# Second layer: each spread, gather, weighting and state release gets its own slot; three engines share the semaphore offsets

## The reference

```python
xa = _ln(x)                                   # then sx = shift(xa) - xa
xxx = jnp.tanh((xa + sx * maa_x) @ maa_w1)    # "hidden", then five mixes
xm = xa[:, :, None] + sx[:, :, None] * (maa_stack + xxx @ maa_w2)
w = exp(-exp(time_decay + jnp.tanh(xw @ td_w1) @ td_w2))
r, k, v, g = xr @ Wr.T, xk @ Wk.T, xv @ Wv.T, silu(xg @ Wg.T)
def step(s, rkvw):                            # over 256 positions
    a = k_t[..., :, None] * v_t[..., None, :]
    out = jnp.einsum('bhi,bhij->bhj', r_t, u * a + s)
    s = a + w_t[..., :, None] * s
    return (s, out)
og = group_norm(out) * g
x1 = x + og @ Wo.T                            # then a feed-forward block:
return x1 + sigmoid(xr2 @ Wfr.T) * (square(relu(xk2 @ Wfk.T)) @ Wfv.T)
```

## Time and profile before

| what | us |
|---|---|
| median of three runs | 4477.55 (4476.36 to 4478.06) |
| the profiled execution's own time | 4474.41 |
| its span, first to last instruction | 4472.4 |
| TensorE busy in the span | 4190.4 |
| VectorE busy | 2937.5 |
| ScalarE busy | 1965.8 |
| GpSimd busy | 1575.5 |

### The profile page before, as it was taken

One profiled execution on the slowest core, in us unless ns is written; L12 is line 12 of the kernel. 1 busy time (PEld: TensorE's weight loads), 2 busy tenths in 40 slices (PEclk: granted clock), 3 DMA queues, 4 the chain that ended last, 5 costly groups with the idle time before them and its releaser, 6 DMA issues. The chain is left out here.

```text
span 4472.4 us, 70619 instructions
## 1 busy us (share of the span) xinstructions
PE 4190.4 (94%) x22096; PEld 3152.1 (70%) x22096; DVE 2937.5 (66%) x6494; ACT 1965.8 (44%) x3814; POOL 1575.5 (35%) x1082
## 2 busy tenths in 40 slices
PE   7999999678999997699999999999999999999999
PEld 3444444356777774488887797887887977888866
DVE  5666665268888887376774775765775756757743
ACT  2555555222333331255553455552555553555522
POOL 1223233146555563133233423333333234232230
PEclk8999999889999998899999999999999999999999
DMA  1000000200000000222222312222312122222122
GB/s 40 25 20 30 20 20 15 118 5 10 15 15 15 15 10 19 74 67 67 72 62 69 102 58 76 67 67 69 98 57 81 58 69 93 63 80 73 51 81 97
DMA packets 128411, 239.77 MB, mean 54 GB/s; under 512 B 16932, under 2 KB 40100, under 8 KB 126896
## 3 DMA queue, kind: packets, MB, share of 16 engines
q1 hardware_dynamic: 126544, 232.99, 16.6%
q0 software_dynamic: 1008, 3.67, 0.2%
q10 hardware_dynamic: 624, 0.18, 0.0%
HBM read 220.79 MB, written 15.73 MB: 53 GB/s over the span
## 5 line engine op out<-in xcount | busy, mean ns | idle before, releaser
L1929 POOL TENSOR_TENSOR c_wl<-c_wr,c_wh 128x512 fp32r<-128x512 f32 (+1 forms) x576 | 819.9, 1435 | 1696.6 <-ACT c_wh L2262 1393.3
L2363 ACT ACTIVATE c_pr<-c_ps,c_nms 128x257 f32<-128x257 f32 x512 | 244.1, 477 | 484.0 <-DVE c_nms L2584 481.7
L581 ACT ACTIVATE a_ex<-a_ps 128x1024 f32<-128x1024 f32 x256 | 261.1, 1023 | 259.8 <-PE a_ps L416 259.7
L692 DVE TENSOR_REDUCE a_nm<-a_ps 128x2 f32<-128x1024 f32 x256 | 311.4, 1221 | 80.9 <-PE a_ps L393 80.8
L1521 DVE TENSOR_TENSOR_SCAN b_sb<-b_wt,b_s,b_ps 128x256 f32<-128x256 f32 x512 | 360.0, 730 | 3.5 <-issue 1.7
L1473 POOL TENSOR_TENSOR b_sb<-b_sb,b_rt 128x1024 f32<-128x1024 f32 x128 | 278.0, 2178 | 185.8 <-DVE b_sb L1521 185.8
L2262 ACT ACTIVATE c_wh<-c_wr 128x512 fp32r<-128x512 f32 (+1 forms) x464 | 315.3, 687 | 47.5 <-PE c_ps L1991 43.5
L1989 PE MATMUL c_ps<-c_hh,c_wh 128*128 128x512 f32 x768 | 310.9, 405 | 12.7 <-DVE c_hl L2468 12.4
L1989 PE MATMUL c_ps<-c_gh,c_wh 128*128 128x512 f32 x768 | 307.2, 400 | 7.1 <-DVE c_gl L2646 4.1
L1991 PE MATMUL c_ps<-c_hh,c_wl 128*128 128x512 f32 x768 | 304.9, 397 | 0.0
L1990 PE MATMUL c_ps<-c_hl,c_wh 128*128 128x512 f32 x768 | 304.3, 396 | 0.0
(11 more groups left out here) (328 smaller groups left out, 10601.8 us busy)
## 6 DMA issues: line engine op xcount, KB each, us to landing
c_wr<-in_downs SPq DMA_DIRECT2D x192, 256.0 KB, 2.7
c_wr<-in_wv SPq DMA_DIRECT2D x64, 512.0 KB, 3.9
c_wr<-in_wk SPq DMA_DIRECT2D x128, 256.0 KB, 2.9
c_wr<-in_wq SPq DMA_DIRECT2D x128, 256.0 KB, 2.6
c_wr<-in_fc SPq DMA_DIRECT2D x64, 256.0 KB, 2.8
b_w<-in_w SPq DMA_DIRECT2D x8, 1024.0 KB, 14.2
a_x<-in_x SPq DMA_DIRECT2D x8, 512.0 KB, 3.9
a_ctx<-in_ctx SPq DMA_DIRECT2D x8, 512.0 KB, 4.2
```

The costliest lines, as they stand in the source:

```text
L581: act.activation(EX[:, n % 4, :, :], ps[:, BT + 2 * (n % 2):BT + 2 * (n % 2) + 2, :], ACT.Exp).then_inc(ex_ready, 1)
L692: dve.tensor_reduce(NM[:, s, :].rearrange("p (h c) -> p h c", h=HG)[:, 2 * p:2 * p + 2, c:c + 1], ps[:, bank:bank + 2, :], AX.X, ALU.max, ...
L1929: pool.tensor_tensor(piece(WL, slot), piece(WR, slot), piece(WH, slot), ALU.subtract).then_inc(piece_cut[slot], 1)
L2363: act.activation(PR[:, i, 0:L + 1], ps[:, BS + 1 - i % 2, 0:L + 1], ACT.Exp, bias=NMS[:, i:i + 1], scale=float(K2) ** -0.5, accum_out=RS[: ...
```

## The change

Four things are changed.

1. The spreads, gathers, weighings and states of the second layer no longer have a formula: each has a slot of its own in a table of 32, 8, 16 and 16 numbers. The two sums have their own as well, and the multiply moves from 4 n - 3 to 4 n - 1.
2. All other numbers of the four tables are new too.
3. `start_ahead` is split in layers 0, 1 and 2: TensorE adds to every third semaphore, VectorE to the next, GpSimd to the rest, after its memsets.
4. In the third layer, SyncE's first context transfer and its six first weight fetches no longer wait.

```diff
@@ layers 0, 1 and 2: tensor, vector, gpsimd (after its memsets)
-            start_ahead(pe, sems)
+            start_ahead(pe, sems[0::3])
+            start_ahead(dve, sems[1::3])
+            start_ahead(pool, sems[2::3])
@@ layer1, tables
-        PE_AT = dict(spread=-29, gather=3, mean=-178, var=-142, hidden=-122, mix=(-119, -116, -114, -103, -98, -86, -80, -73, -67, -56),
...
+        PE_AT = dict(
+                     spread=(-39, -36, -35, -34, -31, -30, -16, -15, -13, -11, -8, -7, -6, 12, 13, 16, 21, 24, 34, 35, 36, 41, 43, 44, 49, 53, 57, 59, 66, 69, 81, 85),
+                     gather=(-13, -10, 18, 39, 47, 60, 91, 107), mean=-180, var=-144, hidden=-130,
...
@@ layer1, loops over the slots
-                    b = due(slot, 4 * pr + PE_AT["spread"])
+                    b = due(slot, PE_AT["spread"][pr])
...
-                    b = due(slot, 16 * o + PE_AT["gather"])
+                    b = due(slot, PE_AT["gather"][o])
...
-                    b = due(slot, 8 * q + POOL_AT["weigh"])
+                    b = due(slot, POOL_AT["weigh"][q])
@@ layer2, sync
-                sp.wait_ge(ct_ready, b + AHEAD)
-                sp.sem_inc(passed, 1)
+                if b > 0:
+                    sp.wait_ge(ct_ready, b + AHEAD)
+                    sp.sem_inc(passed, 1)
...
-                sp.wait_ge(piece_cut[slot], count + AHEAD)
-                sp.sem_inc(passed, 1)
+                if not first:
+                    sp.wait_ge(piece_cut[slot], count + AHEAD)
+                    sp.sem_inc(passed, 1)
```

More of the change, by code:

```diff
@@ L989, in layer1 @@
-        POOL_AT = dict(weigh=-20, scale=-142, shift=-135, mix=(-124, -116, -86, -69, -64), rk=(-82, -71), gate=-44, gated=133, scale2=178,
-                       shift2=189)
-        DVE_AT = dict(multiply=-3, sums=80, mean=-127, inverse=-115, blend=-108, mix=(-98, -96, -91, -81, -66, -61, -54, -47, -41, -30),
-                      v=(-32, -26), gm=(144, 146), ginverse=154, bb=(159, 162), wo=(180, 188), mean2=192, inverse2=200, fkin=221, frin=225,
-                      fv=(262, 270), out=276)
@@ L1640, in _ @@
                 for i in range(2):
-                    b = due(slot, 64 * i + DVE_AT["sums"])
+                    b = due(slot, DVE_AT["sums"][i])
                     if b is not None:
```

34 lines of the change are left out of this document (22 added, 12 removed).

## The result

| kernel | median us | runs | lowest to highest |
|---|---|---|---|
| before | 4476.36 | 5 | 4473.71 to 4478.06 |
| changed | 4454.17 | 5 | 4447.10 to 4454.75 |

The changed kernel is 22.2 us faster: ratio 0.9946, 95% interval 0.9933 to 0.9960. Its profiled execution is the fastest of its five, 4447.10 (span 4445.4), so against the 4474.41 of the profile before 27.3 us are to be placed. The medians differ by 22.2, so 5 of the 27.3 belong to that one execution.

The account below looks back on a forecast made before the run. TensorE was taken to bound the middle batches, VectorE the last, serial chains around them. Terms -4.0 - 0.5 - 3.0 - 11.5 - 5.4 + 5.5 - 2.5 = -21.4 gave 4453.0, as a median 4456; range 4441 to 4472.

Parts of the forecast that it names:

- batches 1 and 2: Second layer: eight more scans done early bring VectorE earlier to v, mean and var; -3.0 us, bounds 0 and -10.
- five middle batches: Second layer: period from hidden to hidden falls to 106.2 us, 2.3 less; -11.5 in all, bounds -20 and -1.
- last batch: Second layer, bound by VectorE: fewer scans and multiplies remain when g ends; -5.4 us, bounds -2 and -8.
- tail, scans' end to gm: Last batch: fkin stands behind seven more scans and two multiplies, so its chain ends later; +5.5 us, bounds +3 and +9.
- start of the third layer: Without SyncE's waits the first transfer and x come earlier, and the mean decides; -2.5 us, bounds -1.0 and -3.4.
- Part 1: Offsets shared by three engines: second layer's first mean 7.0 us earlier, constants hold part back, -4.0; third layer -2.5.
- Part 3: Middle batches: g to hidden becomes 22.7 to 24.9 us, hidden to g 81.6 plus new waits of 0 to 1.8; -11.5.
- Rival A: TensorE never waits in the middle: five periods of 104.3 us, 4447 in all; chance 0.17.
- rival B: The middle keeps its pace, chain and new waits replacing the old: period 108.3 us, 4467 in all; chance 0.22.
- Rival C: Slower: TensorE waits 3.5 us each middle batch at the second gather, then runs at lower clock; 4494; chance 0.04.
- Rival D: The offsets don't help: GpSimd's additions or queues shared with x hold both layer starts; 4463; chance 0.10.
- Rival E: Blend on VectorE meets GpSimd's weighings in the second layer: +4.5 us, 4461; chance 0.07.

Follow-up runs that it names:

- offsets_only: The kernel before with its own slots, plus only the shared offsets and the third layer's removed waits: 4467.67 us, ratio 0.9979 to the kernel before.
- constants_later: The changed kernel with VectorE's work on the constants behind the first batch's reciprocal instead of ahead: 4450.19 us, ratio 0.9936 to the kernel before.
- mean_later: The changed kernel with VectorE's mean of the next batch behind three more scans and a multiply: 4472.20 us, ratio 0.9995 to the kernel before.
- tables_only: The changed kernel's new slots, but TensorE adds all offsets and the third layer's waits stay: 4460.39 us, ratio 0.9961 to the kernel before.
- spreads_again: The changed kernel with four spreads issued twice in each of batches 1 to 6: 4453.84 us, ratio 0.9951 to the kernel before.
- vector_7_gathers_late: The changed kernel with four extra VectorE reciprocals and the last two gathers later on TensorE, all in the last batch: 4452.68 us, ratio 0.9951.

## Why the prediction was right, point by point

The forecast was 4456, the median is 4454.2. The terms, in the profiled execution:

| term | predicted | measured | where |
|---|---|---|---|
| start of the second layer | -4.0 | -3.7 | first transfer to hidden, 30.9 to 27.2 |
| first batch's chain | -0.5 | -0.2 | first to second hidden |
| batches 1 and 2 | -3.0 | -2.5 | second to third hidden; about 0 in six other profiles |
| five middle batches | -11.5 | -13.7 | third to eighth hidden |
| last batch | -5.4 | -7.1 | +3.1 to g, -10.2 for the scans |
| tail, scans' end to gm | +5.5 | +6.1 | |
| behind gm | 0 | +2.5 | lower clock in var2 and fk; -0.4 to -0.1 in three other profiles |
| start of the third layer | -2.5 | -1.7 | last `out` to mean |
| behind that mean | 0 | -3.4 | -4.7 in offsets_only; other meetings of VectorE with GpSimd |
| first layer | 0 | -3.3 | mostly the clock of this execution |

**In part luck: the sum.** The measured terms make -27.0 and the forecast ones -21.4. The median is within 2 us of the forecast although the profile's terms are 6 us beyond it, since the profiled execution was 7 us faster than the median. By the runs of the two halves, the slots gave 17.1 us (14.9 forecast) and the offsets 9.8 (6.5 forecast). A term that was not there (batches 1 and 2) stands against one that was not foreseen (behind the third layer's mean), while the start of the second layer and the middle came out in size (-3.7 for -4.0, -13.7 for -11.5).

**Right, and shown.** Part 1: the mean came as soon as x had landed, and the constants stopped half of that gain; constants_later gives it back. Part 3: of the two pieces of a period the first went from 28.1 to 23.2 (22.7 to 24.9 foretold), the second from 80.4 to 82.7 (81.6 and up to 1.8 more); that the chain through mean sets this pace is shown by mean_later, which takes the whole gain away; that its queue alone made the gain is not shown, since all other slots are new too. Rival A (104.3) and rival B (108.3) both fall: 105.8, where one wait on gv and one on hidden stayed. Rival C's wait of the second gather didn't come, the clock in the middle stayed at 1.00. Rival D falls by offsets_only. Rival E falls as well where it was set up, in the second layer. The lines of blend, and of fkin and frin, in the changed kernel (minimum, median and maximum in ns of one of four instructions):

```profile
L1558 DVE SCALAR_TENSOR_TENSOR b_za<-b_sxa,b_vec,b_xpa x20: 476/480/485, 1138.7 to 1563.3; 128x256 f32<-128x256 f32 x20
```

```profile
L1623 DVE SCALAR_TENSOR_TENSOR b_zb<-b_sxb,b_vec,b_xpb x28: 477/479/485, 1093.6 to 1714.0; 128x256 f32<-128x256 f32 x28
L1623 DVE SCALAR_TENSOR_TENSOR b_sqb<-b_sxb,b_vec,b_xpb x28: 473/477/481, 1100.9 to 1718.4; 128x256 f32<-128x256 f32 x28
```

None is longer than 485 ns, and none overlaps a weighing; in the trace before one of them did (1739.72, frin) and took 1394 ns. The Trainium skill's page SBUF — State Buffer (section "SBUF: two separate sides") lets whichever starts first keep the shared port for its whole instruction. That case agrees in kind: it ended 0.28 us after the weighing did, though alone it takes 0.47. In the third layer the changed kernel does meet such cases (above).

**Mis-sized: batches 1 and 2.** The -3.0 has no counterpart in the runs; the -2.5 of the one profile did not come back. "VectorE comes earlier to v, mean and var" did not shorten anything: in tables_only the time between these hidden products is 95.7 us, before 95.4. I take it that the chain from gate to hidden kept all of it; no run tests that by itself.

**Wrong in its reason: the bound of the middle.** "TensorE is the bound" rested on its busy share. spreads_again added 0.94 us a batch and lost 0.34 to 0.40. mean_later added no work and lost 3.3 for a delay of 2.9, so the middle is bound by a ring of in-order waits between TensorE, VectorE, GpSimd and ScalarE that the mean is a link of; no other link was delayed by itself.

**Wrong in its reason: the tail.** "fkin now stands behind seven more scans and two more multiplies" is true of the order, but no one waited for that: GpSimd's difference, which fkin reads, ended at 1712.77 and fkin started at 1712.81. What grew is the distance from the scans' end to gm, because from g on the scans end 10.2 us earlier (80.6 instead of 90.8) and gm only 4.1 (98.4 instead of 102.5), 3.0 of them by fkin (66.9 instead of 69.9). That the size was right is luck in part: the slots by which fkin moved back are the ones by which the scans moved forward, and I had priced them as a delay of fkin. The last batch isn't VectorE's alone either: vector_7_gathers_late adds 7 us to VectorE for little or nothing.

**Mis-sized, and wrong in its reason: the third layer.** The -2.5 was priced for "without the waits", and the mean came 1.7 earlier. Alone, the removed waits bring the mean 0.9 earlier and VectorE's first use of it 0.4; the shared additions alone bring 1.2 and 1.6. In the whole time the removed waits can't be told from nothing (2.7 us and a loss of 2.2 by the ratios).

**Priced at nothing without a reason: what follows that mean.** It gave 3.4 us here and 4.7 in offsets_only. Every profile with shared additions has some of it (2601.4 to 2608.1 us from that mean to the end, against 2609.5 to 2610.3 with one adder). Set side by side, offsets_only gains on the kernel before 1.0 us by the first mean's clock, is 7 to 8 us ahead near 3190 us (counted from the mean on), gives 4 of them back by 3420, and the large steps stand where a small VectorE instruction meets GpSimd in one kernel and not in the other. How much of the rest is clock alone, I have not taken apart.

## What to carry to other kernels

A wait that one engine shows may be the queue of another: before taking it away, ask who raises the counter, and whether that engine is itself late for the same reason. With tables of slots, an instruction that is placed too early can cost as much as one that is late, because everything behind it in the queue waits too: mean, inverse and blend three to four slots earlier, with the halved gate, cost 5.6 us a period, twice what the whole change had gained there. Judge a bound by adding a known amount of work to it, not by its busy share. And when the start of a long stretch moves, look behind it for short instructions that now meet another engine's long ones: here that was worth as much as the start itself, and it is not a gain to count on in the next version.
